# Decoder kernel on one core: the rotated query product, from TensorE with exchanged weights to VectorE writes to exchanged partitions

## The reference

```python
def _rope(x, L):
    half = x.shape[-1] // 2
    inv_freq = 1.0 / 10000.0 ** (jnp.arange(half) / half)
    ang = jnp.arange(L)[:, None] * inv_freq
    cos, sin = (jnp.cos(ang), jnp.sin(ang))
    x1, x2 = (x[..., :half], x[..., half:])
    return jnp.concatenate([x1 * cos - x2 * sin, x1 * sin + x2 * cos], axis=-1)
```

## Time and profile before

| what | value |
|---|---|
| time, median of 3 runs | 701.72 us (700.37 to 703.38) |
| span of the profiled execution | 699.1 us |
| TensorE busy | 653.7 us (94%), 4654 matmuls |
| VectorE busy | 477.9 us (68%), 1097 instructions |
| ScalarE busy | 353.0 us (50%), 815 |
| GpSimd busy | 355.7 us (51%), 482 |
| share of the last-ending chain | PE 72%, DVE 19%, ACT 4%, issue 2% |
| rotations on VectorE, L1590 and L1591 | 32 each, 13.3 and 13.2 us |
| mean granted TensorE clock | 0.988 |

### The profile page before, as it was taken

How to read it: one execution, slowest core, us unless ns; L and a number is a source line. 1 busy time by engine, 2 the same in 40 slices (tenths; PEclk the granted TensorE clock), 3 DMA queues, 4 the chain that set the end, 5 groups by cost and what they waited for, 6 DMA issues and landing times.

```text
span 699.1 us, 12877 instructions
## 1 busy us (share of the span) xinstructions
PE 653.7 (94%) x4654; PEld 515.7 (74%) x4654; DVE 477.9 (68%) x1097; ACT 353.0 (50%) x815; POOL 355.7 (51%) x482
## 2 busy tenths in 40 slices
PE   9989989889999888789999999999999999999994
PEld 6856668858576545457888888887579888888884
DVE  6578878494284999998866767775375556666555
ACT  4655536150635746356877877776452222222224
POOL 5325416671102795555786766766424444444421
PEclk9999999999999999899999999999999999999998
DMA  8000007001003000000000200000102111111001
GB/s 283 2 2 3 1 2 300 1 1 50 1 0 86 16 1 0 2 1 1 1 2 1 69 1 2 2 1 2 68 24 68 46 45 46 46 46 46 0 1 61
DMA packets 10352, 23.32 MB, mean 33 GB/s; under 512 B 2033, under 2 KB 5074, under 8 KB 9906
## 3 DMA queue, kind: packets, MB, share of 16 engines
q1 hardware_dynamic: 10002, 22.24, 9.7%
q10 hardware_dynamic: 288, 0.26, 0.1%
HBM read 21.45 MB, written 1.05 MB: 32 GB/s over the span
## 4 chain that ended last, share of the span: by engine, by line
PE 72%; DVE 19%; ACT 4%; issue 2%; POOL 1%; DMA 1%; POOLq 0%; SPq 0%; DVEq 0%; ACTq 0%
PE psum L463 43%; DVE A L1555 7%; PE psum L1126 5%; PE psum L1137 4%; PE psum L524 4%; DVE A_rounded L1480 2%; PE psum L577 2%; PE psum L946 2%; PE psum L619 1%; DVE A L1404 1%; DVE stats L1277 1%; DVE x_tok L1274 1%; PE psum L583 1%; PE psum L593 1%; PE psum L956 1%
## 5 line engine op out<-in xcount | busy, mean ns | idle before, releaser
L463 PE MATMUL psum<-parts 128*128 128x256 f32 (+2 forms) x1472 | 253.7, 327 | 2.4 <-DVE C L1591 1.1
L463 PEld LDWEIGHTS psum<-parts 128*128 128x128 f32 (+1 forms) x1472 | 219.9, 190 | 31.5 <-issue 3.9
L2198 POOL TENSOR_SCALAR probs<-probs,row_rec 128x256 f32<-128x256 f32 x128 | 70.1, 560 | 47.5 <-DVE row_rec L1348 44.5
L2112 ACT ACTIVATE A<-psum 128x512 f32<-128x512 f32 x44 | 26.3, 598 | 115.5 <-PE psum L463 115.5
L1784 ACT ACTIVATE probs<-probs,neg_max 128x256 f32<-128x256 f32 x128 | 63.8, 500 | 32.8 <-DVE neg_max L1339 32.8
L1555 DVE TENSOR_TENSOR_SCAN A<-decay,psum 128x256 f32<-128x256 f32 x128 | 75.4, 661 | 4.9 <-PE psum L946 4.9
L1674 DVE TENSOR_TENSOR A<-A,psum 128x512 f32<-128x512 f32 x44 | 30.1, 687 | 70.6 <-ACT A L2112 58.4
L1339 DVE CUSTOM_DVE_ANT_0 probs<-psum,ctxT 128x256 f32<-128x256 f32 x128 | 48.9, 419 | 38.9 <-PE psum L463 36.7
L463 PE MATMUL psum<-parts,A_rounded 128*128 128x256 f32 x404 | 65.3, 288 | 3.5 <-DVE A_rounded L1480 3.5
L463 PEld LDWEIGHTS psum<-parts,A_rounded 128*128 128x128 f32 x404 | 56.3, 196 | 4.9 <-DVE A_rounded L1480 2.8
L1712 DVE TENSOR_TENSOR parts<-A,parts 128x512 fp32r<-128x512 f32 x44 | 48.9, 1111 | 0.8 <-ACT parts L2119 0.7
(11 more groups left out here) (265 smaller groups left out, 1280.9 us busy)
## 6 DMA issues: line engine op xcount, KB each, us to landing
A<-in_experts SPq DMA_DIRECT2D x12, 384.0 KB, 3.1
C<-in_experts SPq DMA_DIRECT2D x10, 384.0 KB, 3.0
A<-in_w_o SPq DMA_DIRECT2D x1, 2048.0 KB, 13.1
x_tok<-in_x_tok SPq DMA_DIRECT2D x1, 1024.0 KB, 7.1
ctxT<-in_ctxT SPq DMA_DIRECT2D x1, 1024.0 KB, 10.7
A<-in_w_uqT SPq DMA_DIRECT2D x1, 768.0 KB, 7.1
out<-x_tok SPq DMA_DIRECT2D x6, 128.0 KB, 1.8
xT<-in_xT SPq DMA_DIRECT2D x2, 256.0 KB, 3.6
```

The source lines that it names most:

```text
L463: ins = mm(o, left[l], right[r], start=first and n == 0, stop=last and n == 2, skip_group_check=True)
L2198: last = pool.tensor_scalar(pr, pr, row_rec[:, u % RING[n], j:j + 1], 1.0, ALU.mult, ALU.mult)
```

## The change

TensorE no longer forms the product with exchanged weights, so `query_pair` issues six matmuls in place of nine. The exchange is made by VectorE: `rotate_pair` multiplies the plain product by the sine table in four instructions of 32 partitions, each of which reads one group of 32 rows and writes to the neighbouring group of `ropes`. They stand ahead of the product with the cosine table, which now is the one that counts `q_mul`. The sine table changes sign, since it is now read at the source's rows. The exchanged weights, their load and their split on GpSimd are gone (`q_split` counts to 2 in place of 3).

```diff
             def query_pair(n):
...
-                product3(rope[:, 0:S], left(wqr_raw_parts), rhs, True, True)
-                product3(rope[:, S:2 * S], left(wqr_swp_parts), rhs, True, True).then_inc(sem("q_rope"), 1)
+                product3(rope[:, 0:S], left(wqr_raw_parts), rhs, True, True).then_inc(sem("q_rope"), 1)
                 product3(lat[:, 0:S], left(qk_parts), rhs, True, True).then_inc(sem("q_l"), 1)
...
+        QUARTERS = ((0, 32), (32, 0), (64, 96), (96, 64))
...
             def rotate_pair(n):
...
-                tt(ropes[:, n % 2, 0:S], rope[:, 0:S], tab_qc, ALU.mult)
-                tt(ropes[:, n % 2, S:2 * S], rope[:, S:2 * S], tab_qs, ALU.mult).then_inc(sem("q_mul"), 1)
+                for to, at in QUARTERS:
+                    tt(ropes[to:to + 32, n % 2, S:2 * S], rope[at:at + 32, 0:S], tab_qs[at:at + 32, :], ALU.mult)
+                tt(ropes[:, n % 2, 0:S], rope[:, 0:S], tab_qc, ALU.mult).then_inc(sem("q_mul"), 1)
...
             load("wqr_raw", wqr_raw)
-            load("wqr_swp", wqr_swp)
...
-                if 25 <= n < 28:
-                    last = split_of(wqr_swp_parts, wqr_swp, n - 25)
-                    if n == 27:
-                        last.then_inc(sem("q_split"), 1)
...
-    o["tab_qs"] = o["tab_ks"] * scale
+    o["tab_qs"] = -o["tab_ks"] * scale
```

More of the change, by code:

```diff
@@ L442, in _, with load_expert @@
             load("tab_qs", tab_qs)
+            def load_expert(c):
+                sp.dma_start(raw[c % RAW], d["experts"][c]).then_inc(sem(f"ld_raw{c % RAW}"), 16)
             sp.wait_ge(sem("fin"), 4 * NT + 1)
-            for c in range(FCH):
-                if c == RAW - 1:
-                    sp.wait_ge(sem("a4_av"), B * NPAIR)
+            for c in range(RAW - 1):
+                load_expert(c)
+            sp.wait_ge(sem("a4_av"), B * NPAIR)
+            for c in range(RAW - 1, FCH):
                 if c >= RAW:
                     sp.wait_ge(sem("m_wd"), c - RAW + 1)
-                sp.dma_start(raw[c % RAW], d["experts"][c]).then_inc(sem(f"ld_raw{c % RAW}"), 16)
+                load_expert(c)
             for i in range(NT - 2):
@@ L560, in heads_of_tile @@
                                     [wqk_parts[:, r, dc, :] for r in range(2)], dc == 0, dc == DC - 1)
-                last.then_inc(sem("qk"), 1)
+                last.then_inc(sem("qkv"), 1)
                 if i == 0:
@@ L568, in heads_of_tile @@
                                     [wv_parts[:, r, dc, :] for r in range(2)], dc == 0, dc == DC - 1)
-                last.then_inc(sem("v"), 1)
+                last.then_inc(sem("qkv"), 1)
             def row_scores(o, qt):
@@ L649, in _ @@
                     loaded(pe, "ident")
-                    pe.wait_ge(sem("const_p"), 1)
+                    pe.wait_ge(sem("const_p"), 2)
                 if i >= 2:
@@ L813, in mixing @@
                 if k < 2:
-                    pe.wait_ge(sem("const_p"), 4)
+                    pe.wait_ge(sem("const_p"), 5)
                     pe.wait_ge(sem("f_alTs"), k + 1)
@@ L1033, in _ @@
                     if n == 5:
-                        pe.wait_ge(sem("const_p"), 3)
+                        pe.wait_ge(sem("const_p"), 4)
                     state_sums(n // 4 - 1)
@@ L1066, in _ @@
                 if n == 29:
-                    pe.wait_ge(sem("q_split"), 3)
+                    pe.wait_ge(sem("q_split"), 2)
                     pe.wait_ge(sem("operand_lo"), QC_AT + 1)
@@ L1168, in product_to @@
                                     [x_parts[:, r, dc, hh] for r in range(2)], dc == 0, dc == DC - 1)
-                last.then_inc(sem(("m_g", "m_u")[w]), 1)
+                last.then_inc(sem("m_gu"), 1)
             def gate_up(place):
@@ L1360, in rotate @@
             def rotate(i):
-                dve.wait_ge(sem("qk"), i + 1)
+                dve.wait_ge(sem("qkv"), 2 * i + 1)
                 if i >= 2:
@@ L1670, in product_of_tile @@
                 dve.wait_ge(sem("m_silu"), place + 1)
-                dve.wait_ge(sem("m_u"), place + 1)
+                dve.wait_ge(sem("m_gu"), 2 * place + 2)
                 if k >= AHEAD:
@@ L1808, in _ @@
                 if i == 0:
-                    act.wait_ge(sem("const_p"), 1)
-                act.wait_ge(sem("v"), i + 1)
+                    act.wait_ge(sem("const_p"), 2)
+                act.wait_ge(sem("qkv"), 2 * i + 2)
                 af(v_sum[:, i, :, 0:HD0], bank[2 + i % 2][:, 0:D].rearrange("p (h w) -> p h w", w=HD0), ACT.Copy
@@ L2107, in silu @@
             def silu(place):
-                act.wait_ge(sem("m_g"), place + 1)
+                act.wait_ge(sem("m_gu"), 2 * place + 1)
                 if place >= 2:
@@ L2458, in laid_out @@
     swp = (r + 32) % 64
-    wqr = a["L1_xattn_W_qr"].reshape(96, 16, 64)
-    o["wqr_raw"] = wqr.reshape(96, 8, 128)
-    o["wqr_swp"] = wqr[:, :, swp].reshape(96, 8, 128)
+    o["wqr_raw"] = a["L1_xattn_W_qr"].reshape(96, 8, 128)
     o["w_dq"] = chunks(a["L1_xattn_W_dq"])
```

16 lines of the change are left out of this document (7 added, 9 removed).

## The result

| | before | after |
|---|---|---|
| time, median of 4 runs each | 701.05 us (699.88 to 703.38) | 715.19 us (714.74 to 716.25) |
| ratio, 95% interval | | 1.0194 (1.0168 to 1.0220) |
| span of the profiled execution | 699.1 us | 713.1 us |
| TensorE busy, matmuls | 653.7 us, 4654 | 651.9 us, 4558 |
| VectorE busy | 477.9 us (68%) | 522.3 us (73%) |

The changed kernel is slower by 14.1 us. The forecast was 708.7 us, 7.0 us more than before, with a range of 698 to 714: the sign held, but the loss is twice the forecast one, and the time lies above the range.

A forecast was written before the change was run, and what follows sets the result against it. VectorE's scans were taken to bound the kernel up to 309.6 us, TensorE from 323.8 to 473.8 us. The terms +4.9, +3.6 and -1.5 gave +7.0 on the 699.1 us span, so a 708.7 us median; range 698 to 714.

The forecast's parts named there:

- TensorE's bound before; three matmuls for 0.36 us a pair: TensorE in the attention loop, almost without gap: each pair drops three of nine matmuls, worth 0.36 us.
- 0.42 us a piece, +1.42 us a rotation: VectorE's rotation: four serial pieces of 0.42 us make it 2.10 us in place of 0.68.
- ScalarE's pair: Two ScalarE copies to different partitions, starting 0.38 us apart, the first lasting 0.36: taken as evidence against overlapping pieces.
- First place: End of the scans: four longer rotations move the first row maxima by 5.7 us and the output product by 4.9.
- ScalarE's slack of 0.73 us: Time between the end of the first scores' exponentials and ScalarE's copy of the state sums, subtracted from 5.7 us.
- Second place: Steps 4 to 17: added VectorE work counts fully until 337.1 us, later comes from its waits; +3.6 us.
- Third place: Steps 18 to 58, 21 pairs: 7.6 us saved on TensorE, 6.1 lost in short periods; -1.5 us.
- The bound around the engines: Steps 18 to 58: low part, five products, GpSimd's sums and ScalarE's copy take 5.1 to 5.2 us, about TensorE's.
- What follows step 58 moves as a whole: Behind the loop's last changed step: nothing changes in length, all of it only shifts.
- Overlap: Rival: pieces start 0.34 us apart, a rotation grows by 1.02 us, together -2.5 us, 699.2 us; chance 0.19.
- The clock: Rival: TensorE idles around the fourth query pair, its clock falls to half, +2 to +4, 712 us; chance 0.12.
- Room for everything: Rival: all added VectorE work falls into its waits, the loop gives 10.1 us, 691.5 us; chance 0.07.

The follow-up runs named there:

- e1: Changed kernel without the exchange of halves: six matmuls a pair and two VectorE products, sine product from plain rows at their own place; 695.47 us.
- e13: Changed kernel with the low part of the second half of the query latents one step later on VectorE (step 12); 714.20 us.
- e7: Changed kernel with VectorE's order turned: the next pair's rotation goes ahead of the low part of the pair before; 715.17 us.
- e9: Kernel before with six matmuls and pieces for query pairs 11 to 31 alone (steps 18 to 58); 705.45 us.
- e3: Changed kernel without the exchange: five products a rotation, all starting at partition 0, three of them on 32 partitions into an unread buffer; 704.95 us.
- e2: Kernel before, nine matmuls a pair kept, with the sine product in four pieces of 32 partitions at their own rows; 714.88 us.
- e12: Kernel before with pieces for pairs 11 to 14, 19 to 22, 27 and 28 alone, and rotation ahead of low part in all steps; 700.31 us.

## Why the prediction missed, step by step

- **TensorE's bound before; three matmuls for 0.36 us a pair.** Right: 5.45 to 5.09 us a period, and 7.5 us over 21 pairs in e1.
- **0.42 us a piece, +1.42 us a rotation.** Right within 0.1 us a rotation: 0.43 to 0.44 from start to start, and four rotations moved the maxima by 6.0 us, 1.50 each. VectorE's busy time rose by 44.4 us in all, 45 forecast. Going by ScalarE's pair was the right choice. The forecast's own remark gave 712 us for 0.43 to 0.44, but 32 rotations at 0.08 us more are 2.6 us at most, of 6.4 that are missing.
- **First place, +4.9.** Right in its mechanism, 5.3 measured: the maxima moved by 6.0 us (318.67 - 306.52 against 312.08 - 305.91), and ScalarE's slack of 0.73 us was used up as written.
- **Second place, +3.6: mis-sized, 5.9 measured.** The step that failed is "later it is taken from the waits". I followed the rotations and let them fill every wait of VectorE. 30.08 us of work plus seven times 1.4 is about 40 us, so 40.3 for the stretch left it no wait at all. But the 2.57 us wait of step 11 is a turn through TensorE and ScalarE within one step: 2.09 us of it stayed, and three waits of 0.26 us for ScalarE came on top. e13 shows 1.3 of the missing 2.3 us. For the other 1.0 there are three candidates, which no run took away alone: the small waits, seven rotations at 0.08 us more (0.6), and low parts of 0.87 in place of 0.67 us (two here, one before).
- **Third place, -1.5: wrong in sign, +1.5 measured.** Four of the five long periods of a block gave 0.36 each as written, the fifth 0.12. The failed step is "of a lag of 3.6 us, the bank and the longer period behind take up all but about 2.2". The three periods behind the long ones take 4.56, 5.85 and 8.47 us (the last two are 407.10 - 401.25 and 415.57 - 407.10), 18.9 in all, where TensorE alone needs 15.3: the lag of 3.6 is paid in full. TensorE stands for the rotation at the front of the third of them, ahead of its 2.75 us of output product:

```profile
409.07 0.95 PE L467 MATMUL psum<-parts 96*128 96x256 f32 x6 [0.99 <-DVE C L1595]
```

```profile
411.41 0.63 PE L528 MATMUL psum<-ident,probs 128*128 128x128 f32 x4 [0.23 <-DVE probsT L1333]
411.87 2.75 PE L1140 MATMUL psum<-vo_fold,A 128*128 128x256 f32 x12
```

  The long product then runs behind the lag instead of over it. VectorE catches up there, TensorE cannot: VectorE, which has worked without a wait since 399.95, waits for TensorE at the next scores.

```profile
416.59 0.42 DVE L1342 CUSTOM_DVE_ANT_0 probs<-psum,ctxT 128x256 f32<-128x256 f32 x1 [0.43 <-PE psum L467]
```

  The bound around the engines, 5.1 to 5.2 us in the forecast and so "about TensorE's", was also too short. In the long periods the low parts start 5.43 us apart, most of them behind a wait for ScalarE, while TensorE goes at 5.09, so VectorE falls behind there already:

```profile
383.45 0.87 DVE L1629 TENSOR_TENSOR A_rounded<-A,A_rounded 128x512 fp32r<-128x512 f32 x1 [0.27 <-ACT A_rounded L2075]
...
388.88 0.87 DVE L1629 TENSOR_TENSOR A_rounded<-A,A_rounded 128x512 fp32r<-128x512 f32 x1 [0.26 <-ACT A_rounded L2075]
...
399.95 0.69 DVE L1629 TENSOR_TENSOR A_rounded<-A,A_rounded 128x512 fp32r<-128x512 f32 x1 [0.26 <-ACT A_rounded L2075]
```

  e7 takes that wait away and gains only 0.2 us a block, so most of the lag is VectorE's own work.
- **What follows step 58 moves as a whole.** Not quite: 0.7 us more behind step 60 (0.8 in e9 alone). Why was not followed.
- **Sum.** 5.3 + 5.9 + 1.5 + 0.7 = 13.4 us; forecast 7.0.
- **Rivals.** Overlap was refuted by the 0.43 us, and e3 shows that its time was off by the same errors: a pitch of 0.34 us would have given 705, not 699. The clock did fall, where it cost nothing, so this sign of a wrong forecast came true without being the cause. Room for everything was refuted; its 691.5 lies below even e1.

## What to carry over

When work moves from the bound engine to another, add it up by stretch for the engine that takes it before following single steps: 30.45 + 11.4 = 41.9 us of VectorE in a block of 42.9 asks for 98% busy, and the chip gave 94%. Waits of that engine are room only if what it waits for comes earlier too; a wait for a turn through two other engines in the same step stays. And a saving on the bound engine is worth its price only in the periods where that engine still ends last: used there alone, the same edit gained 0.6% in place of losing 1.9%.

## What the runs showed of the hardware

- Five VectorE instructions of 256 columns from PSUM start 0.43 to 0.44 us apart when the start partition changes from one to the next, 0.31 to 0.34 when it doesn't, at 32 as at 128 partitions (e3; the kernel before, 0.31 between the scans).
- The low part (128x512, no input from PSUM) takes 0.67 to 0.69 us, but 0.87 in half of the places (kernel after, mean 771 ns of 23 between 360 and 490 us). The length goes with where it starts against GpSimd's products on `probs`. It is 0.87 where it starts 0.6 us behind the first of them, as at 388.88, and 0.69 where it starts 0.8 us behind it, as at 399.95 (GpSimd's timeline below). It is 0.67 where it starts ahead of them. No run changed this alone, so the cause is not shown.

```profile
388.28 2.27 POOL L2202 TENSOR_SCALAR probs<-probs,row_rec 128x256 f32<-128x256 f32 x4
...
399.16 2.29 POOL L2202 TENSOR_SCALAR probs<-probs,row_rec 128x256 f32<-128x256 f32 x4
```

- The first rotation came at 311 us in the profiles of e2, e3, e9 and e13, and at 305 to 308 in the others, with the same work before it. In those four the granted clock of the first 40 us is 0.91, in e12 (307.6 us) 0.96, in the nine others 1.00. What sets it was not tried.
